# Expert bias as the operand of four silus, a dense down product in pieces, and a new order of work

## What is computed

```python
h = clip(exp(min(d_t * A, 2)) * h + clip(d_t * B_t, -2, 2) * x_t, -100, 100)   # 16 states, 1024 steps
y = sum(h * C_t, states) + x_t * D_param
routing = softmax(y @ Wr + br); e = argmax(routing)
hid = silu(y @ up_w[e] + up_b[e])                  # 128 -> 512
moe = (hid @ down_w[e] + down_b[e]) * max(routing) # 512 -> 128
attn = layernorm(x + (layernorm(y + moe) * ln_w + ln_b))
out = layernorm(attn + (silu(attn @ wg) * (attn @ wu)) @ wd)   # 128 -> 384 -> 128, dequantized by 1/127
```

## Time and profile before

| | |
|---|---|
| runs | 981.39, 979.82, 976.91 us |
| median | 979.82 us |
| profiled execution, its own time | 977.01 us |
| its span in the trace | 975.0 us |
| mean granted TensorE clock | 0.824 of full speed |
| TensorE busy | 687.9 us, 71% |
| VectorE busy | 705.7 us, 72% |
| ScalarE busy | 501.3 us, 51% |
| GpSimd busy | 612.3 us, 63% |

### The profile page before, as it was taken

How to read it: one execution, slowest core, us unless ns; L and a number is a source line. 1 busy time by engine, 2 the same in 40 slices (tenths; PEclk the granted TensorE clock), 3 DMA queues, 4 the chain that set the end, 5 groups by cost and what they waited for, 6 DMA issues and landing times.

```text
span 975.0 us, 14730 instructions
## 1 busy us (share of the span) xinstructions
PE 687.9 (71%) x4648; PEld 549.3 (56%) x4648; DVE 705.7 (72%) x1330; ACT 501.3 (51%) x776; POOL 612.3 (63%) x516
## 2 busy tenths in 40 slices
PE   3465747884899579865997499838985798179244
PEld 1233526762687459743985288626873597158233
DVE  3699999789878988698868977898789764311131
ACT  5563354374664747384739474746643463054222
POOL 0376446468864889388948795689648874550540
PEclk8676877996799779985999599967996699579667
DMA  3333435844485527553765367444845373235100
GB/s 118 108 133 108 144 119 173 278 145 146 144 251 169 189 87 232 198 166 109 239 196 174 124 217 240 145 143 136 262 153 180 108 246 115 89 94 180 41 1 22
DMA packets 82086, 149.17 MB, mean 153 GB/s; under 512 B 9404, under 2 KB 51132, under 8 KB 81992
## 3 DMA queue, kind: packets, MB, share of 16 engines
q1 hardware_dynamic: 69192, 134.97, 42.6%
q0 software_dynamic: 4096, 8.40, 2.6%
q10 hardware_dynamic: 8704, 4.72, 1.8%
HBM read 132.64 MB, written 15.40 MB: 152 GB/s over the span
## 4 chain that ended last, share of the span: by engine, by line
PE 28%; POOL 22%; DVE 19%; issue 16%; ACT 6%; DMA 5%; SPq 1%; POOLq 0%; DVEq 0%; ACTq 0%
DVE state L1133 9%; POOL prod L1160 8%; PE psU L636 5%; DMA weights<-in_w_pack 4%; PE psT L652 4%; POOL rstd L1203 4%; PE psD L691 3%; PE psY L525 3%; DVE moe L1075 3%; POOL rows_in L1181 3%; PE psU L677 2%; DVE psB L1124 2%; PE psB L519 2%; PE psU L678 2%; DVE bst L1092 1%
## 5 line engine op out<-in xcount | busy, mean ns | idle before, releaser
L1160 POOL TENSOR_TENSOR prod<-state,c_wide 128x1024 f32<-128x1024 f32 x128 | 312.2, 2444 | 174.6 <-DVE state L1133 156.9
L519 PE MATMUL psB<-parts,sel 128*128 128x512 bf16 x256 | 110.4, 447 | 146.1 <-DVE state L1133 141.8
L1124 DVE TENSOR_TENSOR psB<-dx,psB 128x512 f32<-128x512 f32 x256 | 167.4, 689 | 34.3 <-PE psB L519 26.3
L1133 DVE TENSOR_TENSOR_SCAN state<-decay,state,psB 128x512 f32<-128x512 f32 x128 | 163.8, 1280 | 14.4 <-DVE state L1133 0.5
L525 PE MATMUL psY<-ident,prod 128*128 128x128 f32 x1024 | 157.9, 308 | 12.4 <-POOL prod L1160 12.4
L1133 DVE TENSOR_TENSOR_SCAN state<-decay,psB 128x512 f32<-128x512 f32 x128 | 155.2, 1213 | 5.1 <-ACT decay L758 4.8
L758 ACT ACTIVATE decay<-delta,a_sb 128x1024 f32<-128x1024 f32 x128 | 140.5, 1141 | 32.8 <-DVE state L1133 27.0
L525 PEld LDWEIGHTS psY<-ident,prod 128*128 128x128 f32 x1024 | 137.5, 160 | 28.7 <-POOL prod L1160 17.1
L519 PEld LDWEIGHTS psB<-parts,sel 128*128 128x128 bf16 x256 | 25.7, 103 | 201.5 <-DVE state L1133 190.3
L636 PE MATMUL psU<-yT_sorted,weights 128*128 128x128 f32 x704 | 126.0, 300 | 8.8 <-DMA weights<-in_w_pack 8.0
L636 PEld LDWEIGHTS psU<-yT_sorted,weights 128*128 128x128 f32 x704 | 111.0, 195 | 17.2 <-DMA weights<-in_w_pack 10.6
(11 more groups left out here) (153 smaller groups left out, 1150.7 us busy)
## 6 DMA issues: line engine op xcount, KB each, us to landing
c_wide<-c_rows SPq DMA_DIRECT2D x128, 512.0 KB
weights<-in_w_pack SPq DMA_DIRECT2D x88, 512.0 KB, 4.7
xT_sb<-in_xT SPq DMA_DIRECT2D x8, 512.0 KB, 3.6
y_sorted<-rows_in SPq DMA_DIRECT2D x16, 256.0 KB, 3.0
xt<-in_x SPq DMA_DIRECT2D x8, 512.0 KB, 4.7
rows_out<-result SPq DMA_DIRECT2D x16, 256.0 KB, 5.5
out<-x ACTq DMA_DIRECT2D x16, 256.0 KB, 4.0
y_sorted<-rows_in SPq DMA_DIRECT2D x8, 192.0 KB, 4.8
```

Source lines behind the costliest of these rows:

```text
L519: pe.matmul(tokens(psB, c, h), sel[:, s, :], parts[:, c.n % 2, h * HALF:h * HALF + c.hw], start=True, stop=True).then_inc(b_ready, 1)
L1124: v.tensor_tensor(tokens(psB, c, h), dx[:, n % 2, h * HALF:h * HALF + c.hw], tokens(psB, c, h), ALU.mult).then_inc(inp_ready, 1)
L1133: v.tensor_tensor_scan(state[:, g % NSTATE, t0:t0 + c.hw], decay[:, g % NDECAY, t0:t0 + c.hw], tokens(psB, c, h), before, ALU.mult, ALU.ad ...
L1160: g_.tensor_tensor(prod[:, g % NPROD, w], state[:, g % NSTATE, w], c_wide[:, g % NC, w], ALU.mult).then_inc(prod_ready, 1)
```

## The change

Five things change.

1. The bias of `up` is no product any more. `weights` gets four more columns, in which the loaded row holds the four 128-value pieces of the expert's bias, one for each partition. A row is then 4112 bytes instead of 4096. `silu k` is four instructions of 128 columns in place of one of 512, each with its column as the per-row bias operand.
2. `up` no longer waits for `blocks_ready`; `down` does, since its bias is still a one-hot product. `bias3` holds only the second bias.
3. `ff_down h` is cut: the residual's product stays in it, and three tasks `ff_part h m` add the part of the hidden features m, each after its own `ff_mul h m`.
4. `combine 0` comes before `slots`, and `combine 1` after `scan 8` instead of after `scan 7`.
5. All five order tables are new. The start of an iteration is also cut at another place, so that the same task can bear another offset.

```diff
-W_COLS = 2 * F
+W_DOWN, W_UPB = F, 2 * F
+W_COLS = 2 * F + NF
...
+            def add_ff(c, h, m):
+                u = f"U{(m + NH) % 2}"
+                pe.wait_ge(drained[u], fills(u, c, ("ff_up", h, m + NH)))
+                for j in range(c.hj):
+                    cols = slice(j * 128, (j + 1) * 128)
+                    mm = pe.matmul(bank["D"][:, cols], hh[:, m, cols], wdn_sb[:, m, :], start=False,
+                                   stop=(m == NH - 1), skip_group_check=True)
+                if m == NH - 1:
+                    mm.then_inc(filled["D"], 1)
...
-                    pe.wait_ge(blocks_ready, 2 * n + 2)
                     for f in range(NF):
-                        cols = slice(f * ROWS, (f + 1) * ROWS)
-                        pe.matmul(bank[u][:, cols], weights[:, q % NW, f * 128:(f + 1) * 128],
-                                  yT_sorted[:, k * ROWS:(k + 1) * ROWS], start=(f == 0), stop=False, skip_group_check=True)
-                        mm = pe.matmul(bank[u][:, cols], bias3[:, f * 128:(f + 1) * 128],
-                                       of_block[:, n % 2, k:k + 1].to_broadcast([96, ROWS]), start=False,
-                                       stop=(f == NF - 1), skip_group_check=True)
+                        mm = pe.matmul(bank[u][:, f * ROWS:(f + 1) * ROWS], weights[:, q % NW, f * 128:(f + 1) * 128],
+                                       yT_sorted[:, k * ROWS:(k + 1) * ROWS], start=True, stop=True)
                     mm.then_inc(filled[u], 1)
...
+                    pe.wait_ge(blocks_ready, 2 * n + 2)
+                    pe.matmul(bank[d][:, 0:D], of_block[:, n % 2, k:k + 1].to_broadcast([96, ROWS]), bias3[:, :],
...
                     fill("D", c, task)
                     for j in range(c.hj):
-                        cols = slice(j * 128, (j + 1) * 128)
-                        pe.matmul(bank["D"][:, cols], ident127[:, :], attn[:, h * NJ + j, :], start=(j == 0), stop=False,
-                                  skip_group_check=True)
-                        for m in range(NH):
-                            mm = pe.matmul(bank["D"][:, cols], hh[:, m, cols], wdn_sb[:, m, :], start=False,
-                                           stop=(m == NH - 1), skip_group_check=True)
-                    mm.then_inc(filled["D"], 1)
+                        pe.matmul(bank["D"][:, j * 128:(j + 1) * 128], ident127[:, :], attn[:, h * NJ + j, :],
+                                  start=(j == 0), stop=False, skip_group_check=True)
...
-                    nc.scalar.activation(hid[:, k % 2, :, :], bank[u][:, :].rearrange("p (f r) -> p f r", f=NF), ACT.Silu
-                                         ).then_inc(drained[u], 1)
+                    for f in range(NF):
+                        ins = nc.scalar.activation(hid[:, k % 2, f, :], bank[u][:, f * ROWS:(f + 1) * ROWS], ACT.Silu,
+                                                   bias=weights[:, q % NW, W_UPB + f:W_UPB + f + 1])
+                    ins.then_inc(drained[u], 1)
...
         up_w, down_w.reshape(E, NF, 128, D).transpose(0, 2, 1, 3).reshape(E, 128, NF * D),
+        a["attn_up_b"].reshape(E, NF, 128).transpose(0, 2, 1),
```

More of the change, by code:

```diff
@@ new lines @@
+    (1, "b_max"), (0, "scan", 9), (0, "scan", 10), (-1, "router_pick"), (-2, "stats", 1, 1), (1, "bc_low"),
+    (0, "scan", 11), (-2, "stats", 0, 2), (1, "bound", 0), (0, "scan", 12), (0, "scan", 13), (1, "dx"),
+    (1, "bound", 1), (1, "over"), (-2, "ff_mul", 1, 0), (-2, "ff_mul", 1, 1), (-2, "ff_mul", 1, 2), (0, "scan", 14),
+    (1, "flag"), (-2, "stats", 1, 2), (0, "scan", 15), (1, "scan", 0), (1, "scan", 1), (1, "scan", 2),
+    (0, "router_shift"), (1, "scan", 3), (-1, "combine", 0), (0, "slots"), (-1, "stats", 0, 0), (1, "scan", 4),
@@ L120 @@
+    (0, "prod", 12),
 ]
 SP_ORDER = [
[L122 to L126 removed]
@@ L128 @@
+    (-2, "weights", 2),
 ]
@@ L179, in exists @@
         return task[1] < c.tiles
[L180 removed]
+    if name in ("x_turn", "x_rest", "x_high", "x_low", "ff_up", "gate", "ff_mul", "ff_down", "ff_part", "norm", "stats", "rstd",
                 "affine", "combine", "b_spread", "bound"):
```

116 lines of the change are left out of this document (53 added, 63 removed).

## The result

The changed kernel takes 948.56 us (944.45 to 952.51 in four runs), the kernel before, run beside it, 978.37 (974.91 to 981.39): ratio 0.969, 95% interval 0.965 to 0.9725. The profiled execution took 944.45 us, its span is 942.3.

A forecast was written before the change was run, and what follows sets the result against it. No engine bounds the kernel, but a ring of waits in three arcs, about 102 us a chunk. -2 - 6 - 6 = -14 from 977.0 gives 963, median 966; own range 958 to 974, with the rivals 949 to 985.

The forecast's parts named there:

- the sum: Whole kernel: -2 for six full chunks, -6 for `delta`, -6 for the end, together -14 us.
- its first term: Six full chunks, each period changing by -0.3 us: -2 us, between +4 and -11.
- three signs of being wrong: Middle period above 103 us; `combine 0` stalling as before and `delta` too; `up 7` waiting over 6 us for its weights.
- The period of a steady chunk: From one `decay 0` to the next, 102.2 us: arcs 1 and 2 +1.4, arc 3 -1.7, so -0.3 us.
- the third arc: From `up 7` to `decay 0`, TensorE full: 18.05 us falls to 16.4, -1.7 us a chunk.
- `delta`: Moved behind scan 7, its 16.2 us of stall counted at about four tenths: -6 us, between 0 and -12.
- arcs 1 and 2: `decay 0` through VectorE and GpSimd until `weights 7` loads: +1.4 us a chunk with `combine 0` blocked, given 6 in 10.
- The silus: Four silus at 1.25 us a block; on the path only `silu 10`: +0.1 to +0.3 a chunk, 0.5 at the end.
- The end: After the last scan: `affine 0` -2.7, last `ff_down` -2.9, `up`s -3.7, `up 3` +2.8, `silu 10` +0.5; together -6 us.
- The wider rows: Rival on `weights` rows of 4112 bytes: loads landing 1 us later would give +6, median 972; no chance given.
- a later `result 4`: Rival: scan 12 slips 2.5 us more, `delta` still stalls, each chunk +2.2, median 987; chance 0.17.
- `combine` free: Rival: `combine 0` always runs unblocked, -1.8 instead of -0.3 us a chunk, median 957; chance 0.10.

The follow-up runs named there:

- the base: The changed kernel run once more, unaltered, to compare the kernels taken from it on one chip: 948.15 us, 0.9661 to the kernel before.
- the later version: The changed kernel with `gather 5` ahead of `prod 3` on GpSimd's queue instead of behind it: 938.09 us, 0.955 to the kernel before.

## Why the prediction was right or wrong

The direction and most of the mechanism were right, the size was half. The step that failed is the sum: its first term took the steady chunk for all of them, and two terms, the split of `bias3` and the place of `slots`, stood at nothing. None of my three signs of being wrong came, since all of them look at a middle chunk.

- **The period of a steady chunk** (-0.3): right, -0.6 and -0.1 in chunks 4 and 5. Its arcs too: `weights 7` 2.9 later (2.4 walked), `combine 0` blocked as I gave it 6 in 10, the third arc 15.6 instead of 16.4. In that arc the products are worth 1.7 us (1.4 forecast) and the parts of `ff_down` 0.4 (none).
- **The sum** "-2 - 6 - 6" failed because I took the steady chunk for all of them. Before, chunks 2, 3 and 6 were 106.4, 103.7 and 105.5 us; now every middle chunk is near 102. I had about 5 us there (three times 0.3, and two thirds of `delta`'s 6) and 10.5 came in these profiles. A stall of `delta` stood in chunks 2 and 6; what made chunk 3 longer I haven't traced.
- **A term was missing.** The split of `bias3` went from 640 to 128 columns, nine instructions in front of `scan 3` of chunk 1: +3.5 us when put back, 3.9 in the profile. It was in the diff and I had costed it at nothing without a sentence.
- **`delta`** (-6, "about four tenths"): the size is right, the reason is not. Moving it alone gave 4.8 us, putting it back cost 6.7. But it was no equal share of three stalls. In the new code there is one, and it is on the path almost whole, 6.6 us in chunk 1. In the old code its one profile shows the opposite: chunk 1 gained nothing, and the gain stands at the two stalls of chunks 2 and 6.
- **`combine 0` and `slots`.** I weighed the move by its steady chunk only, between +1.4 and -1.8 us for arcs 1 and 2 together. Put back it costs 11 us, some 6 for `combine 0` though it is stretched in its new place, and 5 for `slots`, which I had not priced: chunk 1, without a `combine`, is 3.8 us shorter for it. That earlier scatters are the way is argued, not shown.
- **The silus** (0.1 to 0.3 a chunk and 0.5): their duration, 1.14 for 1.25, was right and the number of them on the path too small: 7.2 us. I had let the load of `weights 7` start the third arc. It no longer ends last there, and the silus ahead of `up 7` cost 0.7 us a chunk between the two.
- **The end** (-6, measured -9.5 and, in the base's profile, -6.9): the affine is worth 1 and not 2.7, the last `ff_down` 1.3 and not 2.9, and `up 3` waits 0.6 and not 2.8. The products are worth 4.6 there (3.7 forecast). What I hadn't seen is that `combine 0` of chunk 6 starts 10.6 us after the last scan instead of 16.3 (11.3 in the base's profile), and `x_turn 0` 5 us earlier. `weights 7` is 5.1 us earlier in the one profile and 2.6 in the other.
- **The rivals.** The wider rows are excluded (0.999), a later `result 4` happened (+2.9) and was paid back. `combine` free is what the later version does, and it is worth 10 us more, about the 9 that the rival had. The low end of the range was also off by its own terms: the free `combine` at 957, less 6 more for `delta`, is 951 and not 949.
- **What stays open**: half of the 6.5 us of the parts, the 2.9 us that chunk 0 takes more, the price of the two table changes a chunk, and how the parts of the gain share it, since their costs when put back come to twice its size.

By the rule of the Trainium skill cited in the prediction (SBUF — State Buffer, Who interferes with whom), `delta` would wait only for the GpSimd instruction under way. The trace differs: 8.87 us, through four of them. The prediction was wrong to say that the 7.56 us before agree: no GpSimd instruction beside it took more than 2.4 us, it lasted through three. The measurement decides. The same section of the Trainium skill lists casts among what can take the pair of ports that both share, and with that the trace agrees: the cast of 4 by 128 values took 2.40 us beside a product and 0.20 without one.

## What to carry to other kernels

Where the period is a ring of waits, walk the first iteration, the last one and each iteration that differs in the profile, not only a steady one: almost all of this gain lay outside the steady ones. Price every line of a diff, also the set-up that runs once; and price a task's place together with what stands behind it on each of the other queues, since moving one entry of one table alone cost 24 us. Look for VectorE instructions with a duration several times their shortest: swapping one GpSimd entry so that a transfer's issue stood beside them was worth as much as a third of the whole change. But a stall's length is not its price: 16 us of them gave 4.8.

## What the runs showed of the hardware

- A VectorE instruction with two inputs in SBUF, started beside a GpSimd product, was not served between the GpSimd instructions that followed without a gap: 8.87 us through the rest of product 6, products 7 and 8 and `bc_rest`, against 1.19 us alone.
- Executions of one program often differ with the clock that TensorE is granted. The first four of the changed kernel: 944.45 us at 0.825, 945.17 at 0.823, 951.94 at 0.807, 952.51 at 0.809. Over 19 runs of the kernel before beside the first experiments, a clock lower by 0.01 goes with 5 us more, with much scatter. It is no law: the five runs of the base, 0.810 to 0.828, lie within 4.3 us and don't follow it. A single profile can't tell 3 us; the changed kernel's two have spans of 942.3 and 949.3 us.
- A 128-column silu with a per-row bias is 370 ns, four in a row 1.14 us.
